# A windowed-attention block on one core: the zeroing of the values buffers moves to GpSimd, and a bias product and filler products change places in the prologue

## The chip, the cores and the metric

The kernel runs on one core of a Trainium2 chip. A core has five engines that run their own instruction streams and meet only at semaphores: TensorE (PE in the profile, with its weight loads shown apart as PEld), VectorE (DVE), ScalarE (ACT), GpSimd (POOL) and SyncE (SP). The metric is the device time of one execution in microseconds (us), taken as the median of several runs.

## The reference

A Swin-style transformer block on `x` of shape (16, 64, 16, 16), in float32:

```
xn = layernorm over channels(x) * g1 + b1
windows of 8x8 tokens of xn, shifted by 4 (a roll)
q, k, v = windows @ in_w.T + in_b            # 8 heads of 8
attn = softmax(q @ k.T / sqrt(8)) @ v
y = x + (attn @ out_w.T + out_b) @ proj_w.T + proj_b    # roll undone
z = layernorm(y) * g2 + b2
out = y + gelu(z @ fc1_w.T + fc1_b) @ fc2_w.T + fc2_b   # hidden 256
```

Each window has 64 tokens, and there are 16 images of 4 windows. The roll and the layout changes are made on the host when the arrays are laid out.

## The kernel before, in words

The 16 images are cut into 8 tiles (`TILES`), each of two images: tile k has 2 x 256 tokens, and both images of it lie side by side in the 128 partitions. Everything is written out by hand, one instruction stream for each engine, with a named semaphore for every dependence. A prologue makes the folded weights and brings the first tiles on their way; then `slot(t)` runs for each tile on every engine, several tiles deep (`AHEAD` = 3).

For one tile the work goes as follows. DVE takes the statistics of the layer norm (`ln1_stats(k)`: four `bn_stats`, four `bn_aggr`), GpSimd makes the reciprocal root (`ln1_rstd(k)`) and scales (`ln1_scale(k)`; for tile 0 DVE does, in `ln1_scale_first`), giving `xhat`. PE transposes it (`x_transpose(k)`) into the PSUM bank `ps_m`, ACT copies it to `xn`, PE projects q, k and v (`project_qk`, `project_v`), ACT copies them to `qk` and `vz`. Copies of q and k in which all heads of a slot but one are zero are made in `masked` by DMAs that SP issues (`mask_heads`); for tile 0 DVE and ACT make them instead (`mask_k_first`, `mask_q_first`), and for tiles 1 and 2 DVE makes half of k's (`mask_k_half`). PE forms the scores and their transposes, DVE finds row maxima (`find_max`), PE subtracts them (`shift_scores`), ACT exponentiates into `probs`, PE weighs the values (`weigh_values`), and so on through the output projection, the second layer norm and the two-layer perceptron.

The change concerns three things in the prologue.

First, the values buffers. `vz` holds five tiles (`VB` = 5) of the values, spread over 32-wide slots: for each head 8 values for either half of the partitions, and two columns of ones (written by `set_ones`) that give the sum of the exponentials. All the rest must be zero. So each of the five buffers is zeroed once; `copy_v(k)` on ACT then writes tile k's values into it and waits for the zeroing. Before the change, buffer 1 is zeroed by DVE (L787), buffers 2 and 3 by ACT (L942), and buffers 0 and 4 by GpSimd (`zero_values`, L1026).

Second, the bias product: one product of the bias `b1` with the input weights (L552, two instructions on PE, into `ps_o`). DVE turns it into `b_qk` (L801), which ACT adds to q and k. On DVE, the order after tile 0's scaling is: `w_qkv` (L799, the folded weights, from the product of the column means L557), `b_qk` (L801), `ln1_stats(2)`, `ln1_stats(3)`, then the masked copies of tile 0's k (L696), for which the first scores wait.

Third, the fillers: `warm_up(n)` issues n products of zeros with zeros (128 columns, two instructions each in the trace), whose results nobody reads.

Tile and line names in the rows are those of the kernel before. Engines take their instructions in program order, and PE too, except that it may load weights ahead of the product before.

Of the kernel before, what the change touches and what calls it, by code (L numbers as in the profile page):

```python
# [19 lines left out]
P = 128  # L20
# [28 lines left out]
def swin_block_kernel(nc, x_tok_d, x_ch_d, early_d, ident_d, late_d, out_d):  # L49
    ctx = ExitStack()  # L50
    with ctx:
# [87 lines left out]
        vz_zeroed_act = sem("vz_zeroed_act")  # L139
        vz_zeroed_dve = sem("vz_zeroed_dve")  # L140
# [119 lines left out]
        def _(pe):  # L260
# [118 lines left out]
            def weigh_values(k, w):  # L379
                pe.wait_ge(probs_done, 2 * k + w + 1)  # L380
                if w == 0:
# [3 lines left out]
                    if k in (0, VB - 1):  # L385
                        pe.wait_ge(vz_set, 4 if k else 2)
# [126 lines left out]
            def slot(t):  # L513
# [32 lines left out]
                if t >= 2:  # L546
# [5 lines left out]
            nc.tensor.matmul(ps_o[:, 0, 0:1], w_in_t[0:C, 0:2 * C], vec[0:C, B1:B1 + 1],  # L552
                             start=True, stop=True).then_inc(bias_product_done, 1)
            warm_up(3)
# [3 lines left out]
                             start=True, stop=True).then_inc(w_in_mean_done, 1)  # L558
            warm_up(1)
            x_transpose(0)  # L560
            warm_up(2)
# [35 lines left out]
        def _(dve):  # L597
# [153 lines left out]
            def slot(t):  # L751
# [21 lines left out]
                if t == 0:  # L773
                    spread_max_dve(1)
                    late_weights()
                    dve.wait_ge(vz_zeroed, 2)
                    set_ones(VB - 1, VB)
# [9 lines left out]
            nc.vector.memset(vz[:, 1].rearrange("q w n h e -> q (w n h e)"), 0.0).then_inc(vz_zeroed_dve, 1)  # L787
# [25 lines left out]
            dve.wait_ge(vz_zeroed, 1)  # L813
            dve.wait_ge(vz_zeroed_dve, 1)
            dve.wait_ge(vz_zeroed_act, 2)
            set_ones(0, VB - 1)
            ln1_stats(5)
            for t in range(TILES):
                slot(t)
# [19 lines left out]
        def _(act):  # L839
# [20 lines left out]
            def copy_v(k):  # L860
                act.wait_ge(v_projected, k + 1)
                if k in (0, VB - 1):
                    act.wait_ge(vz_zeroed, 2 if k else 1)
                elif k == 1:
                    act.wait_ge(vz_zeroed_dve, 1)
                elif k < VB:
                    act.wait_ge(vz_zeroed_act, k - 1)
                if k >= VB:
# [71 lines left out]
            act.wait_ge(zeros_set, 1)  # L940
            for b in (2, 3):
                nc.scalar.activation(vz[:, b].rearrange("q w n h e -> q (w n h e)"), zeros[:, 0:1].to_broadcast([P, 1024]),  # L942
                                     ACT.Copy).then_inc(vz_zeroed_act, 1)
# [33 lines left out]
        def _(pool):  # L977
# [66 lines left out]
            zero_values(0)  # L1044
# [4 lines left out]
            pool.wait_ge(early_loaded, 16)  # L1049
            ln1_rstd(2)  # L1050
            ln1_scale(2)
            pool.wait_ge(max_found, 1)
# [3 lines left out]
            zero_values(VB - 1)  # L1056
# [64 lines left out]
```

## Time and profile before

| | |
|---|---|
| median of 3 runs | 90.37 us (90.3 to 90.78) |
| the profiled execution's own time | 91.13 us |
| its span, first to last instruction | 89.3 us |
| PE busy | 83.3 us, 93% of the span |
| DVE busy | 64.8 us, 73% |
| ACT busy | 50.0 us, 56% |
| POOL busy | 43.9 us, 49% |
| chain that ended last | PE 80%, DVE 9%, DMA 3%, issue 3%, ACT 2% |

The chain is the trail of work that ended last, followed back from the last instruction to what released it at each step. It lies on PE for four fifths of the span, and most of DVE's share of it lies in the prologue.

### The profile page before, as it was taken

What the parts mean: (1) busy time and instruction counts of PE and PEld (TensorE: products, weight loads), DVE (VectorE), ACT (ScalarE), POOL (GpSimd) and SP (SyncE); (2) the same over time, 40 slices, a digit from 0 to 9 for tenths busy, and PEclk for the clock granted to TensorE, in tenths of its full rate; (3) what the DMA queues carried; (4) which work ended last, traced back from release to release, by engine and by line L of the source; (5) the groups of instructions that cost most, each with busy time, mean ns of one, the idle gap of its engine ahead of it and who ended that gap; (6) DMA issues with size and microseconds to landing.
All of it is one profiled execution on the core that took longest, in us unless ns stands there. A gap on an engine that the chain in (4) does not pass through costs nothing.

```text
span 89.3 us, 4248 instructions
## 1 busy us (share of the span) xinstructions
PE 83.3 (93%) x1794; PEld 52.6 (59%) x1794; DVE 64.8 (73%) x186; ACT 50.0 (56%) x83; POOL 43.9 (49%) x54
## 2 busy tenths in 40 slices
PE   5999999899999999999999999989998999999960
PEld 5986746566676576577666577546637444143420
DVE  4999999898999799669848898996552754333160
ACT  0494998863678196287285264414419966353500
POOL 7988829988007435931920943536703525800000
PEclk9999999999999999999999999999999999999998
DMA  1899400110111111011111100000000000030233
GB/s 21 219 369 421 169 22 0 62 51 29 59 37 44 65 34 64 27 54 46 50 46 51 64 31 22 7 7 0 7 0 7 0 0 0 0 125 31 86 138 100
DMA packets 3620, 5.74 MB, mean 64 GB/s; under 512 B 1073, under 2 KB 1841, under 8 KB 3473
## 3 DMA queue, kind: packets, MB, share of 16 engines
q1 hardware_dynamic: 2736, 3.08, 10.2%
q10 hardware_dynamic: 864, 2.38, 7.1%
q8 instruction: 14, 0.23, 1.1%
q14 instruction: 6, 0.04, 0.2%
HBM read 2.64 MB, written 1.05 MB: 41 GB/s over the span
## 4 chain that ended last, share of the span: by engine, by line
PE 80%; DVE 9%; DMA 3%; issue 3%; ACT 2%; SPq 1%; DVEq 0%
PE ps_s L310 15%; PE ps_u L392 9%; PE ps_t L375 8%; PE ps_t L263 6%; PE ps_u L467 5%; PE ps_o L408 4%; PE ps_m L285 4%; PE ps_s L451 4%; PE ps_t L310 4%; PE ps_t L451 3%; DMA masked<-qk 3%; DVE row_max L628 3%; PE ps_o L420 2%; PE ps_m L451 2%; PE ps_o L467 2%
## 5 line engine op out<-in xcount | busy, mean ns | idle before, releaser
L881 ACT ACTIVATE probs<-ps_t 128x1024 f32<-128x1024 f32 x13 | 13.3, 1025 | 13.2 <-PE ps_t L375 13.0
L628 DVE TENSOR_REDUCE row_max<-ps_s 128x16 f32<-128x1024 f32 x15 | 18.3, 1219 | 2.8 <-PE ps_s L310 2.3
L310 PE MATMUL ps_s<-masked,qk 32*64 32x256 f32 x240 | 16.4, 386 | 1.2 <-DVE row_max L628 0.5
L310 PE MATMUL ps_t<-masked,qk 32*64 32x256 f32 x224 | 15.3, 387 | 0.0
L1005 POOL TENSOR_TENSOR max_x<-max_t,early 128x512 fp32r<-128x512 f32 x6 | 6.7, 1119 | 13.7 <-DVE max_t L636 13.7
L1014 POOL TENSOR_TENSOR rstd<-y_var,minus_half 128x4 f32<-128x4 f32 x8 | 8.3, 1032 | 8.7 <-DVE y_var L682 8.7
L392 PE MATMUL ps_u<-probs,vz 128*32 128x64 f32 x512 | 10.5, 222 | 0.3 <-ACT probs L881 0.3
L310 PEld LDWEIGHTS ps_s<-masked,qk 32*64 32x64 f32 x240 | 8.0, 131 | 3.9 <-issue 1.2
L392 PEld LDWEIGHTS ps_u<-probs,vz 128*32 128x32 f32 x512 | 7.9, 109 | 4.0 <-issue 3.4
L375 PE MATMUL ps_t<-max_x,minus_sel 128*128 128x512 f32 x26 | 9.4, 444 | 0.0
L990 POOL TENSOR_TENSOR rstd<-var,minus_half 128x4 f32<-128x4 f32 x8 | 8.7, 1088 | 1.0 <-DVE var L616 0.4
L263 PE MATMUL ps_t<-zeros 128*128 128x128 f32 x32 | 7.0, 385 | 1.0 <-DVE zeros L784 1.0
L642 DVE STREAM_TRANSPOSE sums<-ps_u 128x512 f32<-128x512 f32 x8 | 5.7, 711 | 2.9 <-PE ps_u L392 2.9
L310 PEld LDWEIGHTS ps_t<-masked,qk 32*64 32x64 f32 x224 | 7.3, 131 | 0.6 <-issue 0.2
L1021 POOL TENSOR_SCALAR rstd_x<-rstd 128x256 f32<-128x256 f32 x8 | 6.9, 857 | 0.7
L263 PEld LDWEIGHTS ps_t<-zeros 128*128 128x128 f32 x32 | 6.2, 286 | 1.1 <-DVE zeros L784 1.0
L887 ACT ACTIVATE y_sq<-y_all 128x256 f32<-128x256 f32 x8 | 3.3, 415 | 5.5 <-DVE y_all L668 5.5
L1039 POOL MEMSET masked<- 128x2048 f32 x3 | 5.4, 1805 | 1.8 <-DVE row_max L628 1.8
L872 ACT ACTIVATE vz<-ps_m 64x256 f32<-64x256 f32 x16 | 6.0, 372 | 0.2
L850 ACT ACTIVATE qk<-ps_m,b_qk 128x512 f32<-128x512 f32 x7 | 4.8, 685 | 2.1 <-PE ps_m L297 2.1
L375 PEld LDWEIGHTS ps_t<-max_x,minus_sel 128*128 128x128 f32 x26 | 3.9, 189 | 3.5 <-issue 1.9
L408 PE MATMUL ps_o<-attn,w_out 128*32 128x128 f32 x128 | 5.4, 273 | 0.2 <-issue 0.2
(110 smaller groups left out, 154.2 us busy)
## 6 DMA issues: line engine op xcount, KB each, us to landing
masked<-qk SPq DMA_DIRECT2D x54, 32.0 KB, 2.2
x_ch<-x_ch_d ACTq DMA_DIRECT2D x1, 1024.0 KB, 8.1
out_d<-result SPq DMA_DIRECT2D x3, 256.0 KB, 2.5
x_tok<-x_tok_d ACTq DMA_DIRECT2D x1, 512.0 KB, 6.1
late<-late_d ACTq DMA_DIRECT2D x1, 352.0 KB, 5.2
x_tok<-x_tok_d SPq DMA_DIRECT2D x2, 128.0 KB, 3.6
x_tok<-x_tok_d ACTq DMA_DIRECT2D x1, 256.0 KB, 4.4
out_d<-result SPq DMA_DIRECT2D x2, 128.0 KB, 2.3
```

The costliest lines, as they stand in the source:

```text
L263: nc.tensor.matmul(ps[:, 0, 0:P], zeros[:], zeros[:], start=True, stop=True)
L310: return nc.tensor.matmul(ps[L * u:L * u + L, g, n * TOK:(n + 1) * TOK], qk[r:r + RG, b, w, t], masked[r:r + RG, b, :, w, t], start=(n == ...
L375: ins = nc.tensor.matmul(scores_t_bank(k, w)[:, g, :], minus_sel[:, 2 * w + g].rearrange("q u j -> q (u j)"), max_x[:, k % 2, :], start=Fa ...
L392: ins = nc.tensor.matmul(u5[32 * h:32 * h + 32, w, n, :, g, :], vz[:, k % VB, w, n, SLOTS * g + h, :], probs[:, w, c:c + L], start=True, s ...
L408: ins = nc.tensor.matmul(o4[32 * j:32 * j + 32, :, u, :], w_out[:, u, c:c + 32], attn[:, w * P:(w + 1) * P], start=True, stop=True, tile_p ...
L451: ins = nc.tensor.matmul(fc1_bank(s, m)[:, w, :], w_fc1[r, m * P:(m + 1) * P], z_all[r, s * STEP:(s + 1) * STEP], start=True, stop=True, t ...
L628: nc.vector.tensor_reduce(row_max[:, 16 * w:16 * w + 16], score_bank(k, w)[:].rearrange("q g (h j) -> q (g h) j", j=L), axis=AX.X, op=ALU. ...
L881: nc.scalar.activation(probs[:, w, :], scores_t_bank(k, w)[:].rearrange("q g c -> q (g c)"), ACT.Exp).then_inc(probs_done, 1)
L990: nc.gpsimd.tensor_tensor(rstd1[:, b, :], var1[:, b, :], minus_half[:], op=ALU.pow).then_inc(x_rstd_done, 1)
L1005: nc.gpsimd.tensor_tensor(max_x[:, k % 2, :].rearrange("q (n i) -> q n i", n=16), max_t[:].unsqueeze(1).to_broadcast([P, 16, 32]), spread1 ...
L1014: nc.gpsimd.tensor_tensor(rstd2[:].rearrange("q n w -> q (n w)"), y_var[:].rearrange("q n w -> q (n w)"), minus_half[:], op=ALU.pow).then_ ...
L1021: nc.gpsimd.tensor_scalar(rstd2_x[:, k % 2].rearrange("q n (w c) -> q n w c", w=2), rstd2[:].unsqueeze(3).to_broadcast([P, BLK, 2, C]), 1. ...
```

## The change

The zeroing of all five `vz` buffers is now GpSimd's: buffer 0 behind `ln1_scale(1)`, buffers 1 and 2 behind `ln1_scale(2)`, buffer 3 behind `ln1_scale(3)`, buffer 4 behind `ln1_scale(4)`. GpSimd no longer zeroes one before its first root, and DVE's and ACT's zeroings are gone. One semaphore counts all five. On DVE the ones are set for buffers 0 to 2 (behind `ln1_stats(5)` instead of before it) and for 3 and 4 in slot 0. On PE the bias product goes from behind the first 8 fillers to behind the first transposes, and the fillers go from 8, 3, 1, 2 to 8 + 2, 2, 1.

```diff
--- before.py
+++ after.py
@@ -136,8 +136,6 @@
         mean_w_set = sem("mean_w_set")
         masked_zeroed = [sem(f"masked_zeroed{i}") for i in range(QB)]
         vz_zeroed = sem("vz_zeroed")
-        vz_zeroed_act = sem("vz_zeroed_act")
-        vz_zeroed_dve = sem("vz_zeroed_dve")
         vz_set = sem("vz_set")
         bias_product_done = sem("bias_product_done")
         b_qk_made = sem("b_qk_made")
@@ -382,7 +380,7 @@
                     pe.wait_ge(v_copied, 2 * k + 2)
                     if k >= 1:
                         pe.wait_ge(sums_transposed, k)
-                    if k in (0, VB - 1):
+                    if k in (0, VB - 2):
                         pe.wait_ge(vz_set, 4 if k else 2)
                 u5 = ps_u[:, 0, :].rearrange("q (w n e g i) -> q w n e g i", w=2, n=BLK, e=2, g=2)
                 for g in range(2):
@@ -549,16 +547,16 @@
             pe.wait_ge(zeros_set, 1)
             warm_up(8)
             pe.wait_ge(early_loaded, 16)
-            nc.tensor.matmul(ps_o[:, 0, 0:1], w_in_t[0:C, 0:2 * C], vec[0:C, B1:B1 + 1],
-                             start=True, stop=True).then_inc(bias_product_done, 1)
-            warm_up(3)
+            warm_up(2)
             pe.wait_ge(mean_w_set, 1)
             pe.wait_ge(w_in_scaled, 1)
             nc.tensor.matmul(ps_u[:, 0, 0:3 * C], mean_w[:], w_scaled[:],
                              start=True, stop=True).then_inc(w_in_mean_done, 1)
+            warm_up(2)
+            x_transpose(0)
+            nc.tensor.matmul(ps_o[:, 0, 0:1], w_in_t[0:C, 0:2 * C], vec[0:C, B1:B1 + 1],
+                             start=True, stop=True).then_inc(bias_product_done, 1)
             warm_up(1)
-            x_transpose(0)
-            warm_up(2)
             pe.wait_ge(w_qkv_made, 1)
             project_qk(0)
             late_products_out()
@@ -773,8 +771,8 @@
                 if t == 0:
                     spread_max_dve(1)
                     late_weights()
-                    dve.wait_ge(vz_zeroed, 2)
-                    set_ones(VB - 1, VB)
+                    dve.wait_ge(vz_zeroed, VB)
+                    set_ones(VB - 2, VB)
                 if tile_ok(t - 1):
                     scale_attn(t - 1)
                     transpose_attn(t - 1)
@@ -784,7 +782,6 @@
             nc.vector.memset(zeros[:], 0.0).then_inc(zeros_set, 1)
             nc.vector.memset(mean_w[:], 1.0 / P).then_inc(mean_w_set, 1)
             nc.vector.memset(masked[:, 0].rearrange("q h w t -> q (h w t)"), 0.0).then_inc(masked_zeroed[0], 1)
-            nc.vector.memset(vz[:, 1].rearrange("q w n h e -> q (w n h e)"), 0.0).then_inc(vz_zeroed_dve, 1)
             ln1_stats(0)
             ln1_var_first()
             dve.wait_ge(early_loaded, 16)
@@ -810,11 +807,9 @@
             spread_max_dve(0)
             mask_k_half(1)
             ln1_stats(4)
-            dve.wait_ge(vz_zeroed, 1)
-            dve.wait_ge(vz_zeroed_dve, 1)
-            dve.wait_ge(vz_zeroed_act, 2)
-            set_ones(0, VB - 1)
             ln1_stats(5)
+            dve.wait_ge(vz_zeroed, VB - 2)
+            set_ones(0, VB - 2)
             for t in range(TILES):
                 slot(t)
             ln2_var(TILES - 3)
@@ -859,13 +854,9 @@
 
             def copy_v(k):
                 act.wait_ge(v_projected, k + 1)
-                if k in (0, VB - 1):
-                    act.wait_ge(vz_zeroed, 2 if k else 1)
-                elif k == 1:
-                    act.wait_ge(vz_zeroed_dve, 1)
-                elif k < VB:
-                    act.wait_ge(vz_zeroed_act, k - 1)
-                if k >= VB:
+                if k < VB:
+                    act.wait_ge(vz_zeroed, k + 1)
+                else:
                     act.wait_ge(values_weighed, 2 * (k - VB) + 2)
                 for u in range(2):
                     r = slice(L * u, L * u + L)
@@ -937,10 +928,6 @@
             act.wait_ge(early_loaded, 16)
             nc.scalar.activation(minus_sel[:].rearrange("q a u j -> q (a u) j"), sel8.unsqueeze(2).to_broadcast([P, 8, L]),
                                  ACT.Copy).then_inc(minus_sel_made, 1)
-            act.wait_ge(zeros_set, 1)
-            for b in (2, 3):
-                nc.scalar.activation(vz[:, b].rearrange("q w n h e -> q (w n h e)"), zeros[:, 0:1].to_broadcast([P, 1024]),
-                                     ACT.Copy).then_inc(vz_zeroed_act, 1)
             copy_xn(0)
             copy_qk_first()
             mask_k_first()
@@ -1041,21 +1028,23 @@
             nc.gpsimd.memset(minus_half[:], -0.5).then_inc(half_set, 1)
             zero_masked(1)
             zero_masked(2)
-            zero_values(0)
             pool.wait_ge(half_set, 1)
             ln1_rstd(0)
             ln1_rstd(1)
             ln1_scale(1)
-            pool.wait_ge(early_loaded, 16)
+            zero_values(0)
             ln1_rstd(2)
             ln1_scale(2)
+            zero_values(1)
+            zero_values(2)
             pool.wait_ge(max_found, 1)
             zero_masked(3)
             ln1_rstd(3)
             ln1_scale(3)
-            zero_values(VB - 1)
+            zero_values(3)
             ln1_rstd(4)
             ln1_scale(4)
+            zero_values(4)
             for t in range(TILES):
                 slot(t)
             for k in range(TILES - 3, TILES):
```

On PE, from the start of the program to the first projection (`ps_t<-zeros` are the fillers, x8 means 8 products of two instructions each; `mean_w` the product of the column means; `ident_sb,xhat` the first transposes; `early` the bias product; `xn,w_qkv` the projection), before:

```order
L263 MATMUL ps_t<-zeros 128x128 x8
L552 MATMUL ps_o<-early 128x1
L263 MATMUL ps_t<-zeros 128x128 x3
L557 MATMUL ps_u<-w_scaled,mean_w 128x192
L263 MATMUL ps_t<-zeros 128x128
L274 MATMUL ps_m<-ident_sb,xhat 128x128 x2
L263 MATMUL ps_t<-zeros 128x128 x2
L285 MATMUL ps_m<-xn,w_qkv 64x256 x4
```

and now:

```order
L261 MATMUL ps_t<-zeros 128x128 x10
L553 MATMUL ps_u<-w_scaled,mean_w 128x192
L261 MATMUL ps_t<-zeros 128x128 x2
L272 MATMUL ps_m<-ident_sb,xhat 128x128 x2
L557 MATMUL ps_o<-early 128x1
L261 MATMUL ps_t<-zeros 128x128
L283 MATMUL ps_m<-xn,w_qkv 64x256 x4
```

The bias product has moved from two places ahead of the column means to directly behind the transposes, and one product of zeros less stands ahead of the projection.

On DVE, from its zeroings to the statistics of tile 2, before:

```order
L786 MEMSET masked 128x2048
L787 MEMSET vz 128x1024
L608 BN_STATS stats<-x_tok 128x6 x4
L611 BN_AGGR mv<-stats 128x2 x4
L616 TENSOR_SCALAR var<-mv 128x4
L791 TENSOR_SCALAR w_scaled<-early 128x64
L793 TENSOR_SCALAR w_scaled<-early 128x128
L608 BN_STATS stats<-x_tok 128x6 x4
L611 BN_AGGR mv<-stats 128x2 x4
L620 TENSOR_TENSOR xhat<-x_tok,rstd 128x256
L799 TENSOR_TENSOR w_qkv<-w_scaled,ps_u 128x192
L801 TENSOR_SCALAR b_qk<-ps_o,early 128x1
```

and now:

```order
L784 MEMSET masked 128x2048
L606 BN_STATS stats<-x_tok 128x6 x4
L609 BN_AGGR mv<-stats 128x2 x4
L614 TENSOR_SCALAR var<-mv 128x4
L788 TENSOR_SCALAR w_scaled<-early 128x64
L790 TENSOR_SCALAR w_scaled<-early 128x128
L606 BN_STATS stats<-x_tok 128x6 x4
L609 BN_AGGR mv<-stats 128x2 x4
L618 TENSOR_TENSOR xhat<-x_tok,rstd 128x256
L796 TENSOR_TENSOR w_qkv<-w_scaled,ps_u 128x192
L798 TENSOR_SCALAR b_qk<-ps_o,early 128x1
```

Only the zeroing of `vz` has gone; `b_qk` keeps its place as the instruction ahead of the statistics of tiles 2 and 3.

On GpSimd, from the scaling of tile 1 to that of tile 3 (`xhat` rows are the scalings, `masked` the zeroing of masked buffer 3), before:

```order
L997 TENSOR_TENSOR xhat<-x_tok,rstd 128x256
L987 TENSOR_SCALAR var<-mv 128x4
L990 TENSOR_TENSOR rstd<-var,minus_half 128x4
L997 TENSOR_TENSOR xhat<-x_tok,rstd 128x256
L1039 MEMSET masked 128x2048
L987 TENSOR_SCALAR var<-mv 128x4
L990 TENSOR_TENSOR rstd<-var,minus_half 128x4
L997 TENSOR_TENSOR xhat<-x_tok,rstd 128x256
L1026 MEMSET vz 128x1024
```

and now:

```order
L984 TENSOR_TENSOR xhat<-x_tok,rstd 128x256
L1013 MEMSET vz 128x1024
L974 TENSOR_SCALAR var<-mv 128x4
L977 TENSOR_TENSOR rstd<-var,minus_half 128x4
L984 TENSOR_TENSOR xhat<-x_tok,rstd 128x256
L1013 MEMSET vz 128x1024 x2
L1026 MEMSET masked 128x2048
L974 TENSOR_SCALAR var<-mv 128x4
L977 TENSOR_TENSOR rstd<-var,minus_half 128x4
L984 TENSOR_TENSOR xhat<-x_tok,rstd 128x256
L1013 MEMSET vz 128x1024
```

Three zeroings of values buffers now stand ahead of the scaling of tile 3, where one stood, and that one ahead of everything shown here.

## Rows read from the trace of the kernel before

**Rows 1.** The chain that ended last: start us, us, what.

```profile
7.17 0.35 DVE w_qkv L799
7.53 0.19 DVE b_qk L801
...
9.58 0.90 DVE masked L696 x3
...
10.52 1.09 PE ps_s L310 x16
...
15.15 2.42 DMA masked<-qk
```

**Rows 2.** Timeline of DVE: start us, us busy, engine, line, operation, tiles, shapes.

```profile
3.43 0.91 DVE L787 MEMSET vz<- 128x1024 f32 x1 [0.16 <-issue]
4.25 0.54 DVE L608 BATCH_NORM_STATS2 stats<-x_tok 128x6 f32<-128x64 f32 x4
...
5.48 0.28 DVE L793 TENSOR_SCALAR w_scaled<-early 128x128 f32<-128x128 f32 x1
5.68 0.60 DVE L608 BATCH_NORM_STATS2 stats<-x_tok 128x6 f32<-128x64 f32 x4
...
6.69 0.43 DVE L620 TENSOR_TENSOR xhat<-x_tok,rstd 128x256 f32<-128x256 f32 x1
...
7.45 0.27 DVE L801 TENSOR_SCALAR b_qk<-ps_o,early 128x1 f32<-128x1 f32 x1
7.63 0.60 DVE L608 BATCH_NORM_STATS2 stats<-x_tok 128x6 f32<-128x64 f32 x4
```

**Rows 3.** Loads of tiles 0 and 1: issue, landing of tile 0, landing of both.

```profile
0.72 0.86 SPq L247 DMA_DIRECT2D x_tok<-x_tok_d  x2
...
x_tok<-x_tok_d SPq DMA_DIRECT2D x1, 128.0 KB, 3.1
...
DMA to landing us min/median/max: 3.1/3.6/4.1
```

**Rows 4.** Timeline of PE's weight loads; 64*128 is the array's tile shape.

```profile
4.75 0.50 PEld L552 LDWEIGHTS ps_o<-early 64*128 64x128 f32 x2 [0.22 <-issue]
...
6.50 0.34 PEld L557 LDWEIGHTS ps_u<-w_scaled,mean_w 128*128 128x128 f32 x2
...
7.17 0.20 PEld L274 LDWEIGHTS ps_m<-ident_sb,xhat 128*128 128x128 f32 x2
7.34 0.53 PEld L263 LDWEIGHTS ps_t<-zeros 128*128 128x128 f32 x4
...
19.01 0.37 PEld L274 LDWEIGHTS ps_m<-ident_sb,xhat 128*128 128x128 f32 x2
...
22.42 0.30 PEld L484 LDWEIGHTS ps_o<-early,late 64*128 64x128 f32 x2
```

**Rows 5.** Timeline of PE's products.

```profile
1.04 3.78 PE L263 MATMUL ps_t<-zeros 128*128 128x128 f32 x16 [1.04 <-DVE zeros L784]
...
7.19 0.42 PE L274 MATMUL ps_m<-ident_sb,xhat 128*128 128x128 f32 x2
...
22.45 0.36 PE L484 MATMUL ps_o<-early,late 64*128 64x1 f32 x2
```

**Rows 6.** Timeline of GpSimd.

```profile
5.57 1.09 POOL L990 TENSOR_TENSOR rstd<-var,minus_half 128x4 f32<-128x4 f32 x1 [0.38 <-DVE var L616]
...
8.35 0.61 POOL L997 TENSOR_TENSOR xhat<-x_tok,rstd 128x256 f32<-128x256 f32 x1
...
12.97 1.80 POOL L1039 MEMSET masked<- 128x2048 f32 x1 [1.76 <-DVE row_max L628]
...
17.29 0.95 POOL L1026 MEMSET vz<- 128x1024 f32 x1
```

**Rows 7.** Timeline of ACT.

```profile
8.89 0.84 ACT L857 ACTIVATE qk<-ps_m,b_qk 128x256 f32<-128x256 f32 x2 [0.86 <-PE ps_m L285]
...
10.57 0.76 ACT L872 ACTIVATE vz<-ps_m 64x256 f32<-64x256 f32 x2
```

## The prediction

> **What bounds the kernel now.** I read the chain that ended last first. After the prologue it is PE without a gap worth naming, so a gain or loss there is one in the instant at which PE starts its steady work, and the prologue's chain is what counts. That chain, in [rows 1], runs over DVE: `w_qkv` at 7.17, `b_qk` at 7.53, the statistics of tiles 2 and 3, the masked copies of tile 0 at 9.58, and only then the first scores on PE at 10.52. Behind those it follows PE, then a copy on ACT, then the masking DMAs of tile 1, from 15.15, and PE's steady work. The reader is to see that between `b_qk` and the masks DVE does nothing but queued statistics: the masks start when DVE gets there. What they need otherwise is there earlier: ACT's first half of tile 0's copy of q and k starts at 8.89, and both halves take 0.84, so the first is done near 9.31 [rows 7], 0.27 before 9.58. So the question is when `b_qk` starts.
>
> Next, the timeline of DVE upstream [rows 2]. The zeroing of `vz` starts at 3.43 and the statistics of tile 0 at 4.25, with no idle time between. Tile 0's scaling runs 6.69 to 7.12, and `w_qkv` follows. On PE [rows 4] the transposes' first weight load is at 7.17, 0.05 behind the scaling's end.
>
> **The change, part by part.**
>
> *DVE's zeroing goes.* It takes 0.91, and 0.82 from start to start. But tile 0's tokens aren't there yet at 3.43: their load is issued at 0.72 and lands 3.1 later, at 3.82 [rows 3]. With the 0.04 or so that a wait takes to be seen (7.12 to 7.17), the statistics start at 3.86 instead of 4.25: 0.39 earlier, not 0.82. Tile 1's load is issued last of the two, near 1.2, and lands 4.1 later, at 5.3 [rows 3]. Its statistics, at 5.68 before, would start at 5.29 [rows 2], so that wait just closes. The root of tile 0 on GpSimd had waited 0.38 for the variance with the engine free [rows 6], so it moves too, from 5.57 to 5.18, and ends at 6.27. Tile 0's scaling on DVE then runs 6.30 to 6.73. **First term: the scaled tile is ready 0.39 earlier.**
>
> *ACT's two zeroings go.* ACT's next work, the copy of the transposes, waited for PE anyway, so this is worth nothing. The same holds for GpSimd's first zeroing: GpSimd waited after it [rows 6].
>
> *PE's order ahead of the transposes.* Before, `w_scaled` was ready at 5.76 [rows 2] while PE came to the column means at 6.50 [rows 4], because it was in its fillers. Sixteen filler instructions took 3.78 [rows 5]. Less the tail of the last one (about 0.42, as the two transposes show, [rows 5]), that is (3.78 - 0.42) / 15 = 0.22 each. Behind the transposes four loads take 0.53 [rows 4], about 0.11 to 0.13 each: by the rows the array runs at half its clock at the start, 1.2 GHz, and at the full 2.4 GHz by about 6.6, whatever the granted clock printed for the whole span. Now twenty filler instructions start from 1.04 at 0.22, to about 5.4, when `w_scaled` is ready (5.76 - 0.39 = 5.37). The means (192 columns, so 1.5 x 0.22 = 0.33, twice) are streamed from about 5.65 to 6.3, and four filler instructions follow, two at 0.22 and two at 0.11, to about 6.95. So the first transpose streams at about 6.9 instead of 7.19, where the scaled tile alone would allow 6.80. **Transposes done: 7.19 + 0.42 = 7.61 before, 7.32 now (at best 7.22).**
>
> *The bias product behind the transposes.* This is what speaks against the change. Before, it was done by 5.3, and `b_qk` started on DVE at 7.45 [rows 2], right behind `w_qkv`. Now `b_qk` must wait for scaling, transposes and bias product in a row. And the bias product uses the array in another shape, 64*128 against 128*128. Where the shape stays, the next weights are loaded early: 7.34 - 7.17 = 0.17 behind the transposes' first load. Where it changes, they are not: ahead of the bias product PE's loads sat idle 0.22, and it came at 4.75, 0.07 before the modelled end of the fillers at 1.04 + 3.78 = 4.82 [rows 4, 5]. At the full clock the nearest twin is L484, of the same shape and one column: from its load at 22.42 to the end of its products at 22.45 + 0.36 = 22.81 is 0.39 [rows 4, 5]. So now: load at 7.32 - 0.07 = 7.25, done at 7.64, seen at 7.68. With the transposes at their best it is 7.58. `b_qk` started at 7.45 before. **Second term: `b_qk` 0.13 to 0.23 later.** Without the wait for the shape, the load would be at the transposes' 6.79 + 0.17 = 6.96, the product done at 7.35, and `b_qk` at 7.39, or 0.06 earlier than before. The Trainium skill's page on TensorEngine Tiling (Array Packing), section Key Properties, states that changing the tiling mode drains TensorE. The idle 0.22 agrees. By that rule the bias product starts behind the transposes' end and the sum is the later one; without it, the earlier.
>
> *Behind `b_qk` nothing absorbs the difference.* From `b_qk` to the statistics of tile 2 takes 0.18 (7.45 to 7.63), from there to the masks 1.95 (to 9.58) [rows 1, 2]. So the masks start at 9.71 to 9.81. ACT's first half, which they also need, moves with the transposes and is early. The scores at 10.52 wait for the masks [rows 1], and the rest of the chain to the masking DMAs has no gap.
>
> *GpSimd's zeroings in their new places.* Each costs 0.95 [rows 6]. The scaling of tile 1 ends at 8.35 + 0.61 - 0.39 = 8.57. Buffer 0 is then zero at 9.52; `copy_v(0)` needs it at 10.57 [rows 7]: 1.05 to spare. Tile 2 took from 8.96 to 11.21 (12.97 less the 1.76 of idle time) [rows 6], so it ends at 11.77. Buffers 1 and 2 end at 13.67, and the zeroing of the masked buffer, at 12.97 before, starts 0.70 later. Tile 3's scaled tokens were ready about 17.3 (the zeroing behind it starts at 17.29), now 18.0; PE's transposes take them at 19.01 [rows 4]: 1.0 to spare. Worth nothing while these last.
>
> *The ones.* The same two writes move behind `ln1_stats(5)`, one buffer's share goes to slot 0, and DVE has the same work ahead of the next row maximum. Nothing.
>
> **Sum.** +0.13 to +0.23, taken as +0.2, nearer the end at which PE's fillers at the half clock count. The profiled span 89.3 becomes 89.5, its own time 91.13 becomes 91.33. The median of the runs lies 0.76 below the profiled one, and 90.37 becomes about 90.55: slower by 0.2%, less than the 0.5% (0.45 us) that a measurement of this kernel can tell from no change.
>
> **The rivals.**
>
> *The shape costs nothing, or `b_qk` doesn't bind.* Then `b_qk` starts 0.06 earlier, and if DVE kept all of the first term, 0.39 earlier. For it: weights are loaded ahead elsewhere (7.17 to 7.34). Against it: the idle 0.22 in front of the old bias product. Times 90.3 to 90.0: between no change and 0.4% faster. Only with a little more would it be faster by over 0.5%, as when tile 0's load lands well before 3.82, but PE's fillers hold the transposes then. Chance 0.25, of which 0.1 beyond the bound.
>
> *The clock rises later: slower.* Fewer fillers, and a product of one column where two fillers were, stand where the array has only just gone to the full clock. Should it still be at the half, the transposes end at about 7.15 + 0.22 + 0.42 = 7.8, the bias product's loads take 0.50 instead of 0.30 [rows 4], so `b_qk` starts near 8.35: 0.9 later, and up to 1.5 if the first projections and scores run at the half too. Time 91.3 to 91.9. It decides once the rise lies past about 7. Against it: the stretch from 4.5 to 6.9 is now denser, with no idle 0.22 and no product of one column. The Trainium skill's TensorE: Matmul & The Clock Gate, Part 1, says that the idle default is 1.2 GHz, that activity releases 2.4, and that the point differs from run to run. The rows of one execution show the rise and can't show its spread. Chance 0.13.
>
> *GpSimd is late: slower.* A zeroing takes longer beside DVE or ACT, and tile 3's scaling passes 19.01. That needs 1.0 us over some 5 us of moved work; the masked buffer, twice a values buffer, takes 1.80 [rows 6], twice 0.90. Then the loss is what passes 1.0, some tenths. Chance 0.04.
>
> *The forecast:* 0.58, with its own range of 90.35 to 90.75.
>
> **How the numbers follow.** The likeliest is 90.55. The range goes down to 90.0, the rival in which DVE keeps the first term, and up to 91.1, about the start of the clock's rival: 0.1 lies below or at the edge, and 0.1 above. Faster by over 0.5%: 0.12 (0.1 of the first rival, and a little spread). Slower by over 0.5%: 0.18 (0.13 of the clock, some of GpSimd, some spread of the forecast's own). Within: 0.70.
>
> **What the profile after would show.** DVE's first statistics at 3.86, tile 0's scaling at 6.30, no DVE `vz` row at 3.43. PE's bias load not at 0.17 behind the transposes' first load but at 0.45, with idle time ahead of it. `b_qk` on DVE with some 0.5 of idle time before it, put down to PE, at 7.58 to 7.68. The masks at 9.7 to 9.8, and the masking DMAs' landing later by the same. On GpSimd the zeroing of the masked buffer at 13.7, and no wait of PE for tile 3. The prediction is wrong if the bias load comes before the transposes' end, if the masks start before 9.58, or if filler instructions at 0.22 stand behind 7.

## The result, and the profile after

The changed kernel takes 95.64 us (median of 4 runs, 95.55 to 95.85) against 90.38 us before: the ratio is 1.058, with a 95% interval of 1.054 to 1.061. It is slower by 5 us where I had said 0.2. (Ratios leave out single executions more than 1.5% above the fastest of their kernel; where that hides something, all runs are given.)

| | after |
|---|---|
| the profiled execution's own time | 95.56 us |
| its span | 93.8 us (before 89.3) |
| PE busy | 86.2 us, 92% |
| DVE, ACT, POOL busy | 64.9, 48.1, 46.4 us |
| mean granted clock | 0.945 (before 0.995) |

DVE is busy as long as before and ACT less; only PE and GpSimd are busier. DVE's timeline, from tile 0's statistics to its first row maximum, answers to [rows 2]:

```profile
3.72 0.60 DVE L606 BATCH_NORM_STATS2 stats<-x_tok 128x6 f32<-128x64 f32 x4 [0.46 <-DMA x_tok<-x_tok_d]
...
6.28 0.39 DVE L618 TENSOR_TENSOR xhat<-x_tok,rstd 128x256 f32<-128x256 f32 x1
...
7.51 0.28 DVE L798 TENSOR_SCALAR b_qk<-ps_o,early 128x1 f32<-128x1 f32 x1 [0.57 <-PE ps_o L557]
7.71 0.59 DVE L606 BATCH_NORM_STATS2 stats<-x_tok 128x6 f32<-128x64 f32 x4
...
9.65 3.83 DVE L694 TENSOR_SCALAR masked<-qk,early 64x256 f32<-64x256 f32 x6
...
13.40 1.20 DVE L626 TENSOR_REDUCE row_max<-ps_s 128x16 f32<-128x1024 f32 x1
```

Down to the start of the masks all is near the forecast: they start at 9.65, against 9.58 before and 9.71 to 9.81 forecast. Then six masked copies take 3.83 us. Before, they ended in time for a row maximum at 11.68, so they took 2.05. The durations of the six show that one copy alone is to blame:

```profile
L694 DVE TENSOR_SCALAR masked<-qk,early x6: 350/362/2508, 9.7 to 11.0; 64x256 f32<-64x256 f32 x6
```

Shortest, median, longest in ns: five take 0.36 us, the last 2.51, from 10.97 to 13.48. GpSimd's timeline of that stretch, which answers to [rows 6]:

```profile
9.76 1.10 POOL L977 TENSOR_TENSOR rstd<-var,minus_half 128x4 f32<-128x4 f32 x1
...
10.95 0.61 POOL L984 TENSOR_TENSOR xhat<-x_tok,rstd 128x256 f32<-128x256 f32 x1
...
11.50 1.84 POOL L1013 MEMSET vz<- 128x1024 f32 x2
...
14.66 1.81 POOL L1026 MEMSET masked<- 128x2048 f32 x1 [1.32 <-DVE row_max L626]
```

The long copy starts when GpSimd's scaling of tile 2 does, at 10.95, and ends 0.14 behind the end of the two zeroings queued directly behind it, at 13.34. The trace of the kernel before had a small one of the same kind, which I had not read:

```profile
L696 DVE TENSOR_SCALAR masked<-qk,early x6: 348/354/724, 9.6 to 11.3; 64x256 f32<-64x256 f32 x6
```

One copy of 0.72 started at 10.64, beside the scaling of tile 2 at 10.59, and ended at 11.36, 0.15 behind the end of that.

Then PE. Its products around the stall, and its busy time and granted clock by stretch (stretch, length, busy, records, clock), first of the kernel after:

```profile
10.59 1.09 PE L308 MATMUL ps_s<-masked,qk 32*64 32x256 f32 x16 [0.50 <-DVE masked L694]
11.62 0.44 PE L272 MATMUL ps_m<-ident_sb,xhat 128*128 128x128 f32 x2
13.53 1.43 PE L308 MATMUL ps_t<-masked,qk 32*64 32x256 f32 x16 [1.48 <-DVE masked L694]
14.89 1.13 PE L283 MATMUL ps_m<-xn,w_qkv 64*64 64x256 f32 x8
```

```profile
10.00:14.00 4.00, 2.02 (x34) 1.00 0.10 39
14.00:24.40 10.40, 10.40 (x117) 0.51 0.06 21
24.40:30.00 5.60, 5.60 (x120) 1.00 0.13 44
```

and of the kernel before, the last of these stretches but one:

```profile
14.00:24.40 10.40, 10.05 (x198) 1.00 0.12 43
```

PE idles 0.50 ahead of the first scores and 1.48 ahead of the second, is busy for only 2.02 of the four microseconds from 10, and from about 14.2 to 24.4 is granted half its clock, 1.2 GHz instead of 2.4. In the same stretch it gets through 117 recorded products instead of 198.

What each part costs can be read from DVE's row maxima, which come in the same order in every version. Each has 16; the third and the eleventh of the kernel before:

```profile
18.78 1.22 DVE L628 TENSOR_REDUCE row_max<-ps_s 128x16 f32<-128x1024 f32 x1
...
43.63 1.23 DVE L628 TENSOR_REDUCE row_max<-ps_s 128x16 f32<-128x1024 f32 x1 [0.18 <-PE ps_s L310]
```

and of the kernel after:

```profile
24.45 1.23 DVE L626 TENSOR_REDUCE row_max<-ps_s 128x16 f32<-128x1024 f32 x1 [3.93 <-PE ps_s L308]
...
49.33 1.23 DVE L626 TENSOR_REDUCE row_max<-ps_s 128x16 f32<-128x1024 f32 x1 [0.15 <-PE ps_s L308]
```

The second scores start at 13.53 instead of 11.91, which is the stall, 1.6. The third row maximum is 5.67 later than before, so the stretch at half the clock adds 4.1. The eleventh is still 5.70 later. The spans differ by only 4.4 at the end, because the traced execution of the kernel before was itself a long one (91.13 against a median of 90.38) and lost 1.3 us more than the changed kernel behind its eleventh row maximum. The medians differ by 5.3.

### The profile page after: what moved, and what is told of

The parts are those of the page before. It is cut to its first block, busy times and chain, and to the rows that moved or that the text cites. A ratio compares the mean times of both kernels' runs of the same rounds, so it can differ in the third digit from the quotient of the medians.

```text
span 93.8 us, 4242 instructions
## 1 busy us (share of the span) xinstructions
PE 86.2 (92%) x1792; PEld 53.1 (57%) x1792; DVE 64.9 (69%) x185; ACT 48.1 (51%) x81; POOL 46.4 (50%) x57
## 4 chain that ended last, share of the span: by engine, by line
PE 82%; DVE 8%; DMA 4%; ACT 1%; issue 1%; SPq 0%
PE ps_s L308 15%; PE ps_u L390 9%; PE ps_t L373 9%; PE ps_t L308 6%; PE ps_m L283 5%; PE ps_u L465 5%; DMA x_tok<-x_tok_d 4%; DVE masked L694 4%; PE ps_o L406 4%; PE ps_s L449 3%; PE ps_t L449 3%; PE ps_m L272 3%; PE ps_o L418 2%; PE ps_m L295 2%; PE ps_m L373 2%; PE ps_m L449 2%
## 5 line engine op out<-in xcount | busy, mean ns | idle before, releaser
L872 ACT ACTIVATE probs<-ps_t 128x1024 f32<-128x1024 f32 x13 | 13.3, 1023 | 14.0 <-PE ps_t L373 13.9
L308 PE MATMUL ps_t<-masked,qk 32*64 32x256 f32 x224 | 17.4, 430 | 1.5 <-DVE masked L694 1.5
L308 PE MATMUL ps_s<-masked,qk 32*64 32x256 f32 x240 | 17.3, 404 | 0.8 <-DVE masked L694 0.5
L373 PE MATMUL ps_t<-max_x,minus_sel 128*128 128x512 f32 x26 | 10.0, 467 | 0.0
L308 PEld LDWEIGHTS ps_t<-masked,qk 32*64 32x64 f32 x224 | 7.8, 142 | 2.6 <-DVE masked L694 1.7
L974 POOL TENSOR_SCALAR var<-mv 128x4 f32<-128x4 f32 x7 | 1.9, 277 | 9.5 <-DVE mv L609 9.2
L261 PE MATMUL ps_t<-zeros 128*128 128x128 f32 x30 | 5.7, 348 | 1.0 <-DVE zeros L782 1.0
L283 PE MATMUL ps_m<-xn,w_qkv 64*64 64x256 f32 x64 | 6.2, 466 | 0.0
L261 PEld LDWEIGHTS ps_t<-zeros 128*128 128x128 f32 x30 | 5.1, 254 | 1.1 <-DVE zeros L782 1.0
```

Of the source, the lines that this page charges most:

```text
L261: nc.tensor.matmul(ps[:, 0, 0:P], zeros[:], zeros[:], start=True, stop=True)
L283: ins = nc.tensor.matmul(ps_m[C * s:C * s + C, w, 0:TOK], w_qkv[r, C * s:C * s + C], xn[r, k % 2, :], start=True, stop=True, tile_position ...
L308: return nc.tensor.matmul(ps[L * u:L * u + L, g, n * TOK:(n + 1) * TOK], qk[r:r + RG, b, w, t], masked[r:r + RG, b, :, w, t], start=(n == ...
L373: ins = nc.tensor.matmul(scores_t_bank(k, w)[:, g, :], minus_sel[:, 2 * w + g].rearrange("q u j -> q (u j)"), max_x[:, k % 2, :], start=Fa ...
L872: nc.scalar.activation(probs[:, w, :], scores_t_bank(k, w)[:].rearrange("q g c -> q (g c)"), ACT.Exp).then_inc(probs_done, 1)
```

## The experiments

The theory after the first look: GpSimd's zeroings hold a port to SBUF that DVE's masked copies need too, PE runs dry, and its clock falls. The rival: PE's new order, with its late bias product and fewer fillers, loses the clock, and the long copy is a side matter.

### One part alone

**e1_zeroing_part** is the changed kernel with PE's lines as before the change; **e8_pe_part** the kernel before with PE's lines as changed:

```diff
             pe.wait_ge(early_loaded, 16)
-            nc.tensor.matmul(ps_o[:, 0, 0:1], w_in_t[0:C, 0:2 * C], vec[0:C, B1:B1 + 1],
-                             start=True, stop=True).then_inc(bias_product_done, 1)
-            warm_up(3)
+            warm_up(2)
...
-            warm_up(1)
+            warm_up(2)
             x_transpose(0)
-            warm_up(2)
+            nc.tensor.matmul(ps_o[:, 0, 0:1], w_in_t[0:C, 0:2 * C], vec[0:C, B1:B1 + 1],
+                             start=True, stop=True).then_inc(bias_product_done, 1)
+            warm_up(1)
```

This is e8 against the kernel before; e1 undoes the same lines in the changed kernel.

Expected of the first: 

> The kernel after the change with PE's old order (bias product behind the first eight fillers, fillers 8, 3, 1, 2); all zeroings on GpSimd as changed. Theory (GpSimd's zeroings of buffers 1 and 2 hold an SBUF port that DVE's last masked copy of tile 0 needs, PE then idles about 1.5 us and falls to half its clock): the last masked copy again takes about 2 us or more, the clock falls near 14, time 95 to 96. Rival (PE's new order, bias product behind the transposes and fewer fillers, costs the clock): time 90 to 90.6, clock full throughout.

Expected of the second: 

> The kernel before with PE's part of the change alone: bias product behind the first transposes, fillers 8 + 2, 2, 1; zeroings as before the change. Theory (port): 90.3 to 90.8, all runs together, with the clock full from about 7. My forecast's second term gives up to 0.5 us more, since here the scaled tile is not earlier: 90.8 to 91.0. Rival (PE's new order costs the clock): 93 to 96, or some of the runs there.

Measured: e1 89.93, ratio 0.990 (0.984 to 0.995), with its four runs at 89.61, 89.80, 90.07 and 95.72, the last with a clock of 0.945. So one run in four came out as expected in time and clock; its copies were not traced. In the profiled one the six copies took 1.70, none over 0.38. GpSimd's root of tile 2 was stretched to 1.25 instead, and its scaling started at 11.23, when the last copy was done. So whether a copy is held seems to depend on who comes first. e8: 91.25, ratio 1.008 (1.005 to 1.011), all seven runs between 91.00 and 91.63 with a clock of 0.998 or more. PE's part alone lost the clock in none of seven runs, but it costs 0.8 us. Its timeline of DVE shows where, against 7.45 and 9.58 of before [rows 1, 2]:

```profile
8.00 0.28 DVE L801 TENSOR_SCALAR b_qk<-ps_o,early 128x1 f32<-128x1 f32 x1 [0.62 <-PE ps_o L559]
...
10.14 2.05 DVE L696 TENSOR_SCALAR masked<-qk,early 64x256 f32<-64x256 f32 x6
```

The masks start 0.56 later, and the eleventh row maximum, at 44.21, is 0.58 later. Where the rest of the 0.8 lies the trace doesn't show.

**e6_changed_again** is the changed kernel, unedited, on another chip. 

> The kernel after the change, unedited, timed again beside the others. If the stall of the last masked copy always happens, all runs lie at 95 to 96. If it depends on who comes first to the port by some tens of nanoseconds, the runs fall in two groups, about 90 to 91 and about 95 to 96.

Its six runs lie at 93.9, 94.0, 94.9, 95.9, 96.4 and 96.5 with clocks of 0.92 to 0.96. Neither forecast fits: it is always slow, if not always equally. In its profiled run the copies took 3.83 again.

### Away from the masked copies

**e2_zeroings_later**: GpSimd's lines behind the scaling of tile 2:

```diff
             ln1_scale(2)
+            pool.wait_ge(max_found, 1)
             zero_values(1)
             zero_values(2)
-            pool.wait_ge(max_found, 1)
-            zero_masked(3)
             ln1_rstd(3)
             ln1_scale(3)
+            zero_masked(3)
             zero_values(3)
```

> The kernel after the change with the zeroings of buffers 1 and 2 behind the wait for the first row maximum, and the zeroing of masked buffer 3 behind tile 3's scaling, so that none of them lies beside the masked copies of tile 0. Theory (port): the six masked copies take about 2.1 us as before, first transposed scores near 12, clock full, time 90.0 to 90.7. Rival (PE's new order): still 95 to 96 with the clock at half for some 10 us.

90.31, ratio 0.994 (0.991 to 0.998). Nine of ten runs lie at 90.1 to 90.6; one, at 93.98, had a clock of 0.944. The copies took 2.06, the longest 0.74, beside the scaling alone.

**e4_wait_for_masks** adds `pool.wait_ge(k_masked_dve, 2)` ahead of `zero_values(1)`. 

> The kernel after the change with one wait more: GpSimd starts the zeroings of buffers 1 and 2 only when the masked copies of tile 0 are done (about 11.7). Theory (port): the masked copies take about 2.1 us, but GpSimd's zeroing of masked buffer 3 now ends near 15.4, and DVE's spreading of the maxima (two SBUF inputs), which would start near 14.7, is held until then: 0.6 to 0.9 us lost there, time 90.9 to 91.4. Rival (only zeroings beside masked copies matter): 90.0 to 90.7. Rival (PE's new order): 95 to 96.

91.02 as a median of all ten, with a ratio of 0.999 (0.995 to 1.003) over those near the fastest. The part about DVE's spreading was wrong: it began at 14.55 and took its usual 0.69 in the middle of the zeroing of the masked buffer (13.70 to 15.51). So this zeroing did not hold an instruction with two SBUF inputs. Of the six runs that kept the clock four lie at 90.8 to 91.04, near the forecast, but for another reason, which is luck. A masked copy for a later tile was held:

```profile
L735 DVE TENSOR_SCALAR masked<-qk,early x4: 470/486/1757, 15.3 to 21.8; 64x512 f32<-64x512 f32 x4
```

It ran from 20.10, beside GpSimd's scaling at 20.08 and the zeroing of buffer 4 at 20.63, and took 1.76 instead of 0.49, again held for both in one piece. The third row maximum is 0.06 later than before, the fourth 0.88. The same copy took 1.45 in e7, 1.49 in e10 and 1.45 in e12. So the change made a second place of this kind. And four of the ten runs had a fallen clock (92.45 to 94.52), though the added wait keeps the zeroings of buffers 1 and 2 off the copies of tile 0; more on that below.

**e7_wait_for_scaling** adds only `pool.wait_ge(x_scaled, 2)` there, GpSimd's wait for its own scaling. 

> The kernel after the change with one wait more on GpSimd: for its own scaling of tile 2 before the zeroings of buffers 1 and 2, a gap of about 0.1 us. Theory A (port kept for a string back to back): a held masked copy is let go at the scaling's end, 0.4 to 0.6 us late at most, and no run lies at 95: all at 90 to 91. Theory B (a zeroing holds the port itself): as the kernel after the change, 95 to 96 wherever it stalls.

90.44, ratio 0.999 (0.996 to 1.002). Eight of twelve runs lie at 90.2 to 90.5 and one at 91.3; one took 94.83 (clock 0.941), and two, at 187 and 407 with the full clock, are unexplained. In the profiled run one copy took 0.74 instead of 2.51: it waited for the scaling (10.92 to 11.53) and got in before the zeroings, which began at 11.59. The run at 94.83 goes against theory A, which had none near 95; it was not traced.

### The port by itself

**e5_port_probe** adds seven trials behind the end of the kernel before. The core of the edit, the seven trials and two of DVE's three kinds:

```diff
+PROBE_POOL = [("scale", "zero", "zero"), ("scale", "wait", "zero", "zero"), ("zero", "zero"), ("scale", "zero", "zero"),
+              ("scale", "zero", "zero"), ("scale", "zero", "zero"), ("zero", "zero")]
+PROBE_DVE = [("mask", False), ("mask", False), ("mask", False), ("mask", True), ("stats", False), ("two", False),
+             ("two", False)]
...
+                    if kind == "mask":
+                        ins = nc.vector.tensor_scalar(probe_d[0:C, i, :], qk[C:P, 0, 0], slot_mask[C:P, i % 4:i % 4 + 1],
+                                                      None, op0=ALU.mult)
+                    elif kind == "two":
+                        ins = nc.vector.tensor_tensor(probe_d[:, i, :], x_tok[:, tokens(0)], x_ch[:, tokens(0)],
+                                                      op=ALU.mult)
```

"scale" is `tensor_tensor` as in `ln1_scale`, "zero" a `memset` of 128x1024, "stats" a `bn_stats`; True means that DVE's first instruction starts GpSimd.

> The kernel before, with seven trials added behind its end, in which GpSimd and VectorE start together on scratch buffers. GpSimd: (1) a scaling and two zeroings of 1024 back to back, (2) the same with a wait of GpSimd for itself between scaling and zeroings, (3) two zeroings alone, (4 to 6) as 1, (7) as 3. VectorE, 6 instructions: (1 to 3) masked copies as those of tile 0, a little behind GpSimd's start, (4) masked copies, the first ahead of GpSimd's start, (5) statistics, (6, 7) products of two SBUF operands. Theory A (GpSimd keeps a shared port for a whole string of instructions back to back that begins with a scaling): the masked copies are held about 2.4 us in 1, only about 0.6 in 2, not at all in 3; in 4 GpSimd's scaling is held and not VectorE; statistics are never held. Theory B (a zeroing holds the port itself): held about 2.4 us in 1 and 2, 1.8 in 3. Theory C (no shared port; something else held the copy): nothing is held in any trial.

One line for each of trials 1, 2, 4, 5, 6 and 7, shortest, median and longest in ns:

```profile
L857 DVE TENSOR_SCALAR probe_d<-qk,early x6: 336/358/2397, 86.6 to 90.0; 64x256 f32<-64x256 f32 x6
...
L857 DVE TENSOR_SCALAR probe_d<-qk,early x6: 222/522/1111, 90.7 to 93.8; 64x256 f32<-64x256 f32 x6
...
L857 DVE TENSOR_SCALAR probe_d<-qk,early x6: 336/532/1114, 97.8 to 101.0; 64x256 f32<-64x256 f32 x6
...
L863 DVE BATCH_NORM_STATS2 probe_d<-x_tok x6: 209/210/227, 101.8 to 102.5; 128x6 f32<-128x64 f32 x6
...
L860 DVE TENSOR_TENSOR probe_d<-x_tok,x_ch x6: 361/411/829, 104.4 to 106.4; 128x256 f32<-128x256 f32 x6
...
L860 DVE TENSOR_TENSOR probe_d<-x_tok,x_ch x6: 361/417/419, 107.3 to 108.9; 128x256 f32<-128x256 f32 x6
```

Theory C is out. In trial 1 one copy is held for a scaling and two zeroings in one piece, as in the changed kernel. In trial 3, zeroings alone, two copies were held, up to 1.11, about one zeroing's length each; so a zeroing holds the port itself, as theory B has it. But B's long holds came in trial 1 alone. In trials 2, 3 and 4 copies get in between GpSimd's instructions, and the longest hold is one zeroing's, whether there is a wait in GpSimd's string (2) or none (3 and 4). So a string without a gap is not always kept in one piece, against theory A too. What decides it no trial shows. So it is likely, but not shown, that the added wait is what let the copy through in e7. In all, the six copies take 3.74 in trial 1 and 3.44 in trial 2: there the loss is shared out rather than removed. Trial 4 refutes A's claim that whoever starts first stays ahead: the first copy ran before GpSimd, and later ones were held all the same. Statistics are not held (0.23 at most), and products of two SBUF inputs only by the scaling (0.83), not by zeroings (0.42 at most). This is how the Trainium skill's SBUF — State Buffer, section SBUF: two separate sides, describes it: an exclusive lock on a port pair between GpSimd and a DVE instruction that is either in a two-port mode or has two SBUF inputs, the latter only against a GpSimd instruction that reads SBUF. The rows agree, kind by kind, if the masked copies are of the two-port kind, which no row shows by itself. The Trainium skill's page gives the lock "for the whole instruction"; in trial 1 it lasted over three.

### The clock

**e3_fillers_in_gap** adds `warm_up(6, ps_u)` between tile 1's transposes and the second scores. 

> The kernel after the change with six more products of zeros between tile 1's transposes and the second scores, where PE stood idle from 12.0 to 13.5. The masked copy is still late. Theory: the stall costs 1.6 to 1.7 us by itself and the fallen clock the rest; with PE busy in the gap the clock stays full and the time is 91.9 to 92.3. Rival (the clock falls for another reason, or the stall is worth the whole loss): time stays at 95 to 96.

92.45, ratio 1.017 (1.011 to 1.023), runs at 92.06, 92.33, 92.58 and 93.46, the clock at 0.996 or more in all of them. No run fell, against ten of ten unfilled. But the profiled run had no held copy (0.38 at most), and the other three were not traced, so it is not shown that a fed PE keeps the clock through a held copy. What it does give is the price of the half clock. Its fillers, 1.50 us of them, put the second scores at 13.42, as late as in the changed kernel (13.53), with the clock at full. Its third row maximum starts at 20.32 against 24.45 there, 4.1 earlier, and its ratio is 1.017 against 1.058.

**e12_wait_filled** is e4 with `warm_up(2, ps_u)` ahead of the first scores. 

> The version in which GpSimd waits for the masked copies, with two more products of zeros ahead of the first scores, where PE stood idle 0.5 us. Of its ten runs without them, four had a fallen clock though no zeroing lay beside the masked copies. Theory D (PE's idle 0.5 us, which the bias product's late place makes, brings the clock near its fall): no run or one in twelve with a fallen clock, time 90.2 to 91.0. Rival (the fall comes from DVE or GpSimd work behind the masked copies, such as the zeroing of the masked buffer beside the copies for tile 1): again three to five runs in twelve at 92 to 95.

90.64, ratio 1.000 (0.998 to 1.002), twelve runs from 90.31 to 91.04, none with a clock under 0.995. Four falls in ten became none in twelve, on another chip, and with the copy for a later tile still held (1.45) in the trace. So the fillers probably did it. But the idle 0.51 ahead of the first scores, which the late bias product leaves, is not enough by itself. It is in e4's trace, of a run that kept the clock, and in e8's, of which no run in seven lost it:

```profile
11.08 1.09 PE L310 MATMUL ps_s<-masked,qk 32*64 32x256 f32 x16 [0.51 <-DVE masked L696]
```

What else e4's four fallen runs had in them is open; none was traced.

### Repairs

**e9_bias_early** is e2 with PE's lines as before the change. **e11_bias_early_regrouped** is the same with fillers 8, 1, 2, 2 instead of 8, 3, 1, 2:

```diff
             nc.tensor.matmul(ps_o[:, 0, 0:1], w_in_t[0:C, 0:2 * C], vec[0:C, B1:B1 + 1],
                              start=True, stop=True).then_inc(bias_product_done, 1)
-            warm_up(3)
+            warm_up(1)
...
-            warm_up(1)
+            warm_up(2)
             x_transpose(0)
```

**e10_act_zeroes** is e11, but ACT zeroes buffers 1 and 2 ahead of its first copy, and the other GpSimd work stays where the change put it. The three expectations, in this order:

> The kernel after the change with both repairs: PE's old order (bias product behind the first eight fillers) and the zeroings of buffers 1 and 2 behind the first row maximum. Theory (the port costs the 5 us, the bias product behind the transposes 0.5 us): masked copies from about 9.4, none held by a zeroing, 89.7 to 90.1, no run near 95. Rival (PE's part of the change is neutral): as the version with late zeroings and PE's new order, 90.1 to 90.6.

> Late zeroings as in the first, and on PE the bias product early, but fillers 8, 1, 2, 2, so that the column means are ready before tile 0's scaled tokens. The folded weights then start near 6.7 instead of 7.0 and the masked copies near 9.1. Theory: 89.4 to 89.8, 0.3 below the first. Rival (the clock's rise needs the fillers): a few tenths to 1 us slower than the first.

> As the next one, but buffers 1 and 2 are zeroed by ACT while it is idle (from about 5.4), and GpSimd zeroes only 0, 3 and 4, in the changed places; PE as in the next one. Theory (only zeroings on GpSimd beside the masked copies hold them): no run near 95, 89.6 to 90.1. Rival (the stall comes from elsewhere, for instance from GpSimd's scaling of tile 2 alone): some runs near 95, as with the changed kernel.

Measured: e9 89.88, ratio 0.992 (0.988 to 0.995), runs 89.2 to 90.4. e11 89.73, ratio 0.991 (0.988 to 0.993), runs 89.4 to 90.1. e10 90.15, ratio 0.996 (0.994 to 0.998), twelve runs from 90.0 to 90.7. No run of the three near 95, and no clock under 0.995. e11's DVE timeline:

```profile
6.08 0.42 DVE L618 TENSOR_TENSOR xhat<-x_tok,rstd 128x256 f32<-128x256 f32 x1
6.42 0.34 DVE L796 TENSOR_TENSOR w_qkv<-w_scaled,ps_u 128x192 f32<-128x192 f32 x1
6.69 0.27 DVE L798 TENSOR_SCALAR b_qk<-ps_o,early 128x1 f32<-128x1 f32 x1
...
8.82 1.93 DVE L694 TENSOR_SCALAR masked<-qk,early 64x256 f32<-64x256 f32 x6
```

The masks start 0.76 earlier than before the change. The first row maximum, at 11.16, is 0.52 earlier, since it now waits for the scores, and the eleventh 0.55. e9's masks did not come at 9.4 as expected but at 9.78, later than before the change, because DVE sat idle 0.87 ahead of `w_qkv` for the column means, which PE took behind its fillers. Its eleventh row maximum, at 43.81, is 0.18 later than before, and yet its median is 0.7 lower. So its gain does not come from the prologue. At least part of it lies at a third place of the same kind, late in the kernel before:

```profile
L652 DVE TENSOR_TENSOR attn_tok<-sums,recip x8: 382/384/1169, 28.7 to 70.2; 128x256 f32<-128x256 f32 x8
```

One of eight products of two SBUF inputs took 1.17 instead of 0.38. It started at 55.20, beside a product of GpSimd that reads SBUF (`max_x`, 55.04 to 56.09). Its like is in e8's trace (1.18) and in none of the other traced versions (0.43 at most), where the two come in another order; from the fourteenth to the last row maximum the two kernels with the hold take 6.12, e9 and e11 5.58. e11 and e9 differ by less than their intervals; both beat the kernel before.

In e10 the masks also start early, at 9.08, but tile 1's tokens happened to land late there (a wait of 0.44 on that load). Its third row maximum is 0.26 behind e11's, its fourth 0.81: the later tile's copy was held there (1.49), beside the scaling and the zeroing of buffer 4, which e10 left in place.

## Why the prediction was wrong

*The step that failed* is "GpSimd's zeroings in their new places ... Worth nothing while these last." I asked only whether each zeroing would be done before its reader. The times I gave for them were near (buffers 1 and 2 to 13.67; measured 13.34), and no reader waited. I did not ask what ran beside them: from 11.5 to 13.3 lay the end of DVE's masked copies, the very instructions on which my chain rested. My rival "GpSimd is late" had contention in it, but only as GpSimd's loss, and priced a zeroing by its own duration (0.90, the same in every row). And the paragraph before it, on what stands behind `b_qk`, took it for granted that the six copies would take as long as before (2.05); they took 3.83. The sign was in the trace of before, in the longest of six copies.

*The clock's rival* had the half clock as its price (up to 91.9; with the stall it was 95.6) and the wrong cause. I had it rise late, near 7. It rose in time, and fell at about 14.2, behind a stretch in which PE was half idle. I had looked for what the fillers do to the rise and not for what idle time does to a clock once risen. The stall of 1.6 us was thus multiplied: 4.1 more, shown by the row maxima above and again by e3, which is as late and has the full clock. That the stall is what made the clock fall rests on the order of events in two traces (the changed kernel and e6, the second with the same 1.48 of idle time) and on the versions without the hold, most of whose runs kept it.

*First term, 0.39 earlier:* right. The statistics began at 3.72 behind the load (0.53 earlier), but tile 1's load then held the next ones to 5.35, so tile 0's scaling was at 6.28 (forecast 6.30). With PE's old order little of this reaches the masks: they start at 9.42 in e1 and 9.78 in e9, against 9.58, since `w_qkv` then waits for the column means.

*Second term, `b_qk` 0.13 to 0.23 later:* the mechanism was right, its size here 0.06: PE got through twenty filler instructions in 3.85, where sixteen took 3.78 [rows 5], so it had the full clock earlier, and the transposes weren't held by fillers. That is luck: in e8 the same twenty took 4.64. The weight loads, which answer to [rows 4]:

```profile
6.72 0.20 PEld L272 LDWEIGHTS ps_m<-ident_sb,xhat 128*128 128x128 f32 x2 [0.47 <-DVE xhat L618]
7.09 0.29 PEld L557 LDWEIGHTS ps_o<-early 64*128 64x128 f32 x2 [0.17 <-issue]
```

0.37 behind the transposes' first load and 0.08 ahead of their modelled end, where a load that keeps the array's shape came 0.17 behind: the change of shape costs about what I said (0.45). By itself (e8), without the first term, the late bias product moved the masks by 0.56 and the end by 0.8; the forecast's terms would give 0.39 + 0.2 = 0.6 for that. *ACT's zeroings worth nothing, the ones nothing:* no trace speaks against it. e1's good runs and e9 are 0.7 to 0.9 us faster than the kernel before, but the prologue explains at most 0.2 of that (the eleventh row maximum is 0.19 earlier in e1 and 0.18 later in e9); the rest lies behind it, and I had not looked there.

What stays open: why one run each of e1, e2 and e7 and four of e4 lost the clock and others of the same kernel did not; what lets a waiting copy in between GpSimd's instructions in one trial and not in another; and e7's two very long runs.

## What to carry to other kernels

When work is moved to GpSimd, look not only at whether it is done in time but at which VectorE instructions run beside it: here masked copies were held by scalings and zeroings, products of two SBUF inputs by GpSimd instructions that read SBUF, and statistics not at all. The longest of a group of equal instructions, beside its median, shows such holds before any change is made. Where the held instruction feeds TensorE, price the stall with the clock it may cost, here 4.1 us on 1.6. A kernel whose outcome hangs on who comes first by a tenth of a microsecond needs all its runs looked at, not the median. And where two versions differ in time, lay the same instruction of both traces side by side along the whole span before a gain is put down to the part that was changed.

## What the runs showed of the hardware that I had not expected

- A string of three GpSimd instructions back to back kept the port for 2.40 us (trial 1) and 2.51 us (the changed kernel); with a wait between them one held copy got through (0.74, e7). In trial 4 the same string without a wait let the copies in between (longest 1.11).
- It works the other way too: where the six copies ran unheld in 1.70, GpSimd's root of tile 2 (128x4) took 1.63 instead of 1.0 to 1.1 (e3, e4), and ended 0.04 behind the last copy.
- A product of two SBUF inputs took 1.17 instead of 0.38 beside a GpSimd product (the kernel before; 1.18 in e8).
- The clock fell in four of e4's ten runs, none of them traced, with the zeroings of buffers 1 and 2 kept off the copies of tile 0. With two filler products ahead of the first scores it fell in none of twelve.
